# Moving two small side tasks of a fused attention and expert kernel on TensorE's slots, and two small VectorE operations in another form

## The reference, cut to what matters

```python
x = x + xattn(ctx, layernorm(x))   # q, k, v projections; 32 sub-heads of 8 dims; softmax over 128 keys
#   att = softmax(q k / sqrt(8)); att = att[:, :, 0] - lam * att[:, :, 1]; out = att @ v
x = x + moe(layernorm(x))
#   shared = silu(x @ ws_gate) * (x @ ws_up) @ ws_down
#   scores = sigmoid(x @ gate_w.T); top 2, weights normalised and times 2.5
#   routed = sum over the two chosen experts of weight * (silu(x @ w_gate) * (x @ w_up)) @ w_down
```

## Time and profile before

| | |
|---|---|
| median of 3 runs | 2349.24 us (2347.07 to 2359.59) |
| the profiled execution's own time | 2360.34 us |
| its span, first to last instruction | 2358.6 us |
| busy: TensorE, VectorE, ScalarE, GpSimd | 86%, 70%, 62%, 59% of the span |
| mean granted TensorE clock | 0.96 |

### The profile page before, as it was taken

One profiled execution on the slowest core, in us unless ns is written; L12 is line 12 of the kernel. 1 busy time (PEld: TensorE's weight loads), 2 busy tenths in 40 slices (PEclk: granted clock), 3 DMA queues, 4 the chain that ended last, 5 costly groups with the idle time before them and its releaser, 6 DMA issues.

```text
span 2358.6 us, 76415 instructions
## 1 busy us (share of the span) xinstructions
PE 2039.5 (86%) x20269; PEld 1421.1 (60%) x20270; DVE 1653.8 (70%) x4770; ACT 1464.0 (62%) x3558; POOL 1381.4 (59%) x2121
## 2 busy tenths in 40 slices
PE   4888888888888889888888888888883799989997
PEld 3555565555555556555555555555552677768886
DVE  3667777788878887888788887888763566644443
ACT  2666666767777777777677776767651344435553
POOL 4355666666666666666666666666643355545665
PEclk8799999999999999999999999999986899989999
DMA  4566556656566656656566565656534799867784
GB/s 136 168 205 195 164 161 166 169 161 173 164 174 170 170 169 170 175 163 171 165 177 167 165 171 166 175 165 172 154 89 152 250 290 293 284 215 237 233 244 144
DMA packets 583280, 432.50 MB, mean 183 GB/s; under 512 B 434070, under 2 KB 507930, under 8 KB 582688
## 3 DMA queue, kind: packets, MB, share of 16 engines
q1 hardware_dynamic: 547872, 342.28, 52.7%
q0 software_dynamic: 30720, 84.99, 9.9%
q10 hardware_dynamic: 4608, 4.26, 0.5%
HBM read 235.18 MB, written 200.47 MB: 185 GB/s over the span
## 4 chain that ended last, share of the span: by engine, by line
PE 52%; DVE 17%; issue 14%; SPq 5%; DMA 5%; ACT 4%; ACTq 1%; DVEq 1%; POOL 1%; POOLq 0%
PE mx_ps L715 9%; PE mx_ps L469 7%; PE ms_ps L551 6%; PE ms_ps L728 5%; DVE mx L917 4%; PE ms_ps L530 4%; PE o_ps L502 4%; PE st_ps L707 3%; DVE mxp L924 3%; DMA stacks<-mxT 2%; PE ms_ps L531 2%; ACT rowt L758 2%; PE ms_ps L532 2%; PE o_ps L513 2%; PE ms_ps L559 2%
## 5 line engine op out<-in xcount | busy, mean ns | idle before, releaser
L917 DVE TENSOR_REDUCE mx<-mx_ps 128x4 f32<-128x512 f32 x1024 | 701.6, 686 | 301.1 <-PE mx_ps L469 291.3
L776 ACT ACTIVATE prob<-st_ps 128x512 f32<-128x512 f32 x1024 | 609.1, 603 | 428.1 <-PE st_ps L462 426.2
L469 PE MATMUL mx_ps<-stacks 48*128 48x128 bf16 x4096 | 400.7, 222 | 34.1 <-DMA stacks<-mxT 24.6
L462 PE MATMUL st_ps<-stacks 50*128 50x128 bf16 x4096 | 397.4, 221 | 0.0
L469 PEld LDWEIGHTS mx_ps<-stacks 48*128 48x128 bf16 x4096 | 233.0, 96 | 196.1 <-issue 104.6
L502 PE MATMUL o_ps<-prob,v_sb 128*32 128x256 f32 x4096 | 330.8, 395 | 1.2 <-ACT oT L767 0.8
L715 PE MATMUL mx_ps<-w_gu_sb,prob 128*128 x1152 | 301.9, 385 | 0.0
L1122 DVE TENSOR_TENSOR prob<-prob,mx_ps 128x128 f32<-128x128 f32 x288 | 83.0, 288 | 221.3 <-ACT prob L859 219.7
L462 PEld LDWEIGHTS st_ps<-stacks 50*128 50x128 bf16 x4096 | 231.4, 95 | 2.2 <-issue 1.1
L1313 POOL DMA_INDIRECT rows_dram<-stacks x144 | 141.5, 983 | 154.2 <-DVE stacks L1116 142.8
L854 ACT ACTIVATE prob<-st_ps 128x256 f32<-128x256 f32 x288 | 110.4, 383 | 159.2 <-PE st_ps L707 152.9
(11 more groups left out here) (199 smaller groups left out, 4948.7 us busy)
## 6 DMA issues: line engine op xcount, KB each, us to landing
stacks<-stack_dram SPq DMA_DIRECT2D x512, 192.0 KB
stacks<-rows_dram SPq DMA_DIRECT2D x144, 260.0 KB
stack_dram<-kp SPq DMA_DIRECT2D x128, 256.0 KB, 3.0
stack_dram<-qp SPq DMA_DIRECT2D x64, 384.0 KB, 3.8
stacks<-rows_dram SPq DMA_DIRECT2D x144, 132.0 KB
stacks<-base_dram SPq DMA_DIRECT2D x144, 128.0 KB
x_in<-in_x SPq DMA_DIRECT2D x64, 256.0 KB
c_in<-in_ctxT SPq DMA_DIRECT2D x64, 256.0 KB, 2.7
```

Source lines behind the costliest of these rows:

```text
L462: return pe.matmul(st_ps[k % 2][:, i * P:(i + 1) * P], k_st[p][64 * h:64 * h + KROWS, u, j, :], q_st[p][64 * h:64 * h + KROWS, u, j, :], s ...
L469: return pe.matmul(mx_ps[k % 2][:, i * P:(i + 1) * P], q_st[p][64 * h:64 * h + ROWS, u, j, :], k_st[p][64 * h:64 * h + ROWS, u, j, :], sta ...
L776: nc.scalar.activation(prob[k % 4][:, :], st_ps[k % 2][:, :], ACT.Exp, scale=float(HALF) ** -0.5).then_inc(a_exp, 1)
L917: v.tensor_reduce(mx[:, u, c * CHUNK:(c + 1) * CHUNK], mx_ps[k % 2][:, :].rearrange("p (c n) -> p c n", c=CHUNK), AX.X, ALU.max).then_inc( ...
```

## The change

Rank sums go from bank TO in slot 9 to bank M0 in slot 11; for that the first half of the key projection goes from slot 11 to slot 13. The turn of the second maxima goes from slot 1 to the end of slot 2, that of the first maxima from slot 11 to slot 10, with ScalarE's copy of the second moved to k = 2 and the tanh of the shared expert from k = 6 to k = 5. VectorE does `places` at k = 12 and `positions` at k = 13 (before 10 and 11); the copy to bf16 becomes a maximum over an axis of length one, and the place of a row a sum of absolute values straight from `hotp`. On GpSimd the query's `split` comes before the first two scatters. SyncE's list is unchanged.

```diff
--- before.py
+++ after.py
@@ -563,9 +563,10 @@
             def clear(it, bank, n):
 
                 a, b, d, r = it.plus(3), it.plus(1), it.plus(-1), it.plus(-2)
-                users = {"M0": (((a_v, 1, b, 1),), ((a_e, 1, r, 1),), ((a_dn, 1, r, 1),), ((a_k, 2, a, 2),)),
+                users = {"M0": (((a_v, 1, b, 1),), ((a_e, 1, r, 1),), ((a_dn, 1, r, 1),), ((v_pf, 1, r, 1),),
+                                ((a_k, 2, a, 2),)),
                          "M1": (((v_x, 1, a, 1),), ((v_sh, 1, r, 1),), ((v_q, 1, a, 1),), ((a_h, 1, d, 1),)),
-                         "TO": (((a_mT, 2, it, 2),), ((v_cb, 4, d, 4),), ((v_cb, 4, it, 1),), ((v_pf, 1, r, 1),),
+                         "TO": (((a_mT, 2, it, 2),), ((v_cb, 4, d, 4),), ((v_cb, 4, it, 1),),
                                 ((a_mT, 2, b, 1),), ((v_cb, 4, it, 2),), ((v_cb, 4, it, 3),))}[bank]
                 for i, user in enumerate(users):
                     if it.k is None or i == (n - 1) % len(users):
@@ -579,15 +580,15 @@
                     clear(it, "M1", 0)
                     wait(pe, a_n1, 2, a, 2)
                     turn(xn, M1, p_xT)
-                if k == 1 and do_c:
-                    clear(it, "TO", 0)
-                    turn_max(it, 1)
                 if k in (1, 2) and do_b:
                     if k == 1:
                         clear(it, "M0", 0)
                     mm = value(b, k - 1)
                     if k == 2:
                         mm.then_inc(p_v, 1)
+                if k == 2 and do_c:
+                    clear(it, "TO", 0)
+                    turn_max(it, 1)
                 if k in (3, 5) and do_r:
                     if k == 3:
                         clear(it, "M1", 1)
@@ -603,7 +604,7 @@
                     turn_out(d, 3)
                 if k in TURN_AT and do_c:
                     h = TURN_AT.index(k)
-                    clear(it, "TO", (2, 5, 6)[h])
+                    clear(it, "TO", (2, 4, 5)[h])
                     turn_out(it, h)
                 if k in (8, 9) and do_r:
                     if k == 8:
@@ -620,20 +621,20 @@
                     mm = project(0, (x_hi, x_lo), M1, k - 9)
                     if k == 10:
                         mm.then_inc(p_q, 1)
-                if k == 9 and do_r:
+                if k == 10 and do_b:
                     clear(it, "TO", 3)
+                    turn_max(b, 0)
+                if k == 11 and do_r:
+                    clear(it, "M0", 3)
                     wait(pe, v_hot, 1, r, 1)
                     flat = hot[:, :, :, :].rearrange("p u k e -> p (u k e)")
-                    pe.matmul(TO[:, 0:2 * E2], upper[:, :], flat, start=True, stop=True)
-                    pe.matmul(TO[:, 2 * E2:4 * E2], onesb[:, :], flat, start=True, stop=True).then_inc(p_pf, 1)
-                if k == 11 and do_b:
-                    clear(it, "TO", 4)
-                    turn_max(b, 0)
-                if k in (11, 14) and do_a:
-                    if k == 11:
-                        clear(it, "M0", 3)
+                    pe.matmul(M0[:, 0:2 * E2], upper[:, :], flat, start=True, stop=True)
+                    pe.matmul(M0[:, 2 * E2:4 * E2], onesb[:, :], flat, start=True, stop=True).then_inc(p_pf, 1)
+                if k in (13, 14) and do_a:
+                    if k == 13:
+                        clear(it, "M0", 4)
                         wait(pe, g_cl, 1, a, 1)
-                    mm = project(1, (c_hi[a.par()], c_lo[a.par()]), M0, (k - 11) // 3)
+                    mm = project(1, (c_hi[a.par()], c_lo[a.par()]), M0, k - 13)
                     if k == 14:
                         mm.then_inc(p_k, 1)
                 if k == 13 and do_d:
@@ -799,7 +800,7 @@
                         nc.scalar.activation(kp[:, 1, :], k_rest[:, :], ACT.Copy).then_inc(a_kb, 1)
                     if k == 5 and do_c:
                         copy_out(it, 0)
-                    if k == 6 and do_r:
+                    if k == 5 and do_r:
                         wait(act, p_su, 1, r, 1)
                         wait(act, v_sg, 1, r)
                         nc.scalar.activation(sh_t[:, :], M1[:, 0:SW], ACT.Tanh, scale=0.5).then_inc(a_sh, 1)
@@ -921,7 +922,8 @@
 
                     wait(dve, v_red, NCH, s, k + 1)
                     wait(dve, p_mT, 2, s)
-                    v.tensor_copy(mxp[:, u, :, 0, :], mx[:, u, :].rearrange("p (h j) -> p h j", h=2)).then_inc(v_mxa, 1)
+                    v.tensor_reduce(mxp[:, u, :, 0, :], mx[:, u, :].rearrange("p (h j one) -> p h j one", h=2, one=1), AX.X,
+                                    ALU.max).then_inc(v_mxa, 1)
                     wait(dve, v_mxa, 1, s, 1)
                     v.tensor_tensor(mxp[:, u, :, 1, :], mx[:, u, :].rearrange("p (h j) -> p h j", h=2), mxp[:, u, :, 0, :],
                                     ALU.subtract).then_inc(v_mx, 1)
@@ -981,9 +983,9 @@
 
 
                 row = rowt[s.par()]
-                tot = TO[:, 2 * E2:4 * E2].rearrange("p (u e) -> p u e", u=2)
-                place = TO[:, 0:2 * E2]
-                both, safe, part = (TO[:, 4 * E2 + 2 * i:4 * E2 + 2 * i + 2] for i in range(3))
+                tot = M0[:, 2 * E2:4 * E2].rearrange("p (u e) -> p u e", u=2)
+                place = M0[:, 0:2 * E2]
+                both, safe, part = (M0[:, 4 * E2 + 2 * i:4 * E2 + 2 * i + 2] for i in range(3))
                 wait(dve, p_pf, 1, s, 1)
                 v.tensor_reduce(both, top[:, :, 0:TOPK], AX.X, ALU.add).then_inc(v_rt, 1)
                 v.tensor_tensor(base[:, 1, :], base[:, 0, :], tot[:, 0, :], ALU.add).then_inc(v_ps, 1)
@@ -1006,11 +1008,12 @@
             def positions(s):
                 row = rowt[s.par()]
                 wait(dve, v_ps, 3, s, 3)
-                v.tensor_reduce(row[:, :, C_POS:C_POS + TOPK], hotp[:, :, :, :], AX.X, ALU.add).then_inc(v_w, 1)
-                wait(dve, v_w, 1, s, 1)
+                v.tensor_reduce(row[:, :, C_POS:C_POS + TOPK], hotp[:, :, :, :], AX.X, ALU.add,
+                                apply_absolute_value=True).then_inc(v_w, 1)
                 wait_par(dve, d_scat, SCAT, s.plus(-2))
-                v.scalar_tensor_tensor(posi[s.par()][:, :], row[:, :, C_POS], -1.0, row[:, :, C_POS], ALU.mult,
-                                       ALU.max).then_inc(v_pos, 1)
+                with nc.allow_low_precision(reason="one place among zeros, a whole number below 2**24"):
+                    v.tensor_reduce(posi[s.par()][:, :], hotp[:, :, 0, :], AX.X, ALU.add,
+                                    apply_absolute_value=True).then_inc(v_pos, 1)
 
             def step(it):
                 a, b, d, xs, r = it.plus(3), it.plus(1), it.plus(-1), it.plus(4), it.plus(-2)
@@ -1038,12 +1041,12 @@
                     if k == 9 and do_d:
                         wait(dve, g_x2, 4, d, 4)
                         stats(d, x2[d.par()], bs2, mv2, v_b2, v_s2, a_n2)
-                    if k == 10 and do_r:
+                    if k == 12 and do_r:
                         places(r)
-                    if k == 11 and do_r:
-                        positions(r)
                     if k == 12 and do_a:
                         rest(a, M1, a_q, qp, q_rest, g_qs, v_q)
+                    if k == 13 and do_r:
+                        positions(r)
 
             steps(dve, step)
 
@@ -1285,15 +1288,16 @@
                     numbers(r)
                 if do_c:
                     residual(it, 0)
+                if do_a:
+                    split(a, q_rest, qp, a_qb, g_qs)
                 if do_r:
                     wait(gp, v_pos, 1, r, 1)
                     wait(gp, v_pf, 1, r, 1)
+                    wait(gp, v_w, 1, r, 1)
                     wait(gp, g_tok, 1, r, -1)
                     scatter(r, 0, 1)
                     wait(gp, g_base, 1, r, 1)
                     scatter(r, 0, 0)
-                if do_a:
-                    split(a, q_rest, qp, a_qb, g_qs)
                 if do_c:
                     residual(it, 1)
                 if do_r:
```

## The result

The changed kernel takes 2523.59 us (median of four, 2509.99 to 2534.66) against 2349.06 us before (four, 2347.07 to 2359.59): 1.073 times as long, 95% interval [1.067, 1.079]. That is 174.5 us more, where I had forecast 94 more, and 3.6 us above my range. Its profiled execution took 2525.35 us, with a span of 2523.6 and a mean granted clock of 0.90 (before 0.96).

A forecast was written before the change was run, and what follows sets the result against it. TensorE's and SyncE's chains were taken as tied; after the change SyncE's sets the period: 4.5 + 23.0 = 27.5 us, plus 0.8 for the clock, 28.3. That is 1.6 us more in 59 iterations: 2349 + 94 = 2443 us, range 2325 to 2520.

The forecast's parts named there:

- The two tied chains: TensorE's work and SyncE's in-order queue close the same loop at nearly equal length; the longer sets the period, 26.6 us.
- the costly one: Second maxima's turn moved to just before slot 3: everything in SyncE's list comes 1.1 us later.
- SyncE's chain at 23.0 us from copy to landing: From ScalarE's copy of the second maxima to the landing of slot 0's last DMA: 23.0 us.
- The copy at 4.5 us with the clock up: ScalarE's copy of the second maxima ends 4.5 us after slot 0 instead of 3.4.
- The clock: One large idle time ahead of slot 0 lowers TensorE's granted clock: 0.8 us per iteration, bounds 0 and 2.7.
- the sum 27.5 + 0.8: Forecast period: 4.5 us to the copy plus 23.0 of SyncE's chain, plus 0.8 for the clock, 28.3 us.
- TensorE alone at 24.3 us: TensorE's own period: 26.7 us less 3.0 of removed waits, plus 0.6 for new ones.
- VectorE's forms: Reduces at L924 and L1012 take about 0.2 us each, saving VectorE 1.1 and 0.8; nothing for the period.
- Rival 2: SyncE's chain has room, TensorE bounds: 2207 us in full, 2278 to 2331 partly; chance 0.19.
- rival 3: No change: SyncE's chain of 22.1 to 22.4 us, period 26.6 to 26.9; chance 0.11.
- rival 4: VectorE's reduce is held up as the cast was: VectorE alters by 1.1 us, the period not; no chance given.
- Rival 1: SyncE's chain bounds and the clock does not fall: 26.9 to 27.5 us per iteration, 2360 to 2396 us; chance 0.20.

The follow-up runs named there:

- e1: Changed kernel with the turn of the second maxima and ScalarE's copy back in slot 1 (k = 1): 2403.51 us, 0.976 of before.
- e2: Kernel before with only the turn of the second maxima moved to the end of slot 2, ScalarE's copy at k = 2: 2526.92 us, 1.026 of before.
- e4: Changed kernel with SyncE's list reordered, second maxima's DMAs between the query and key puts: 2319.94 us, 0.947 of before.
- e4b: Repeat of the changed kernel with SyncE's list reordered: 2301.40 us, 0.936 of before.
- f3: Changed kernel with SyncE's list reordered, beside the changed kernel on one long chip: 2323.27 us, 0.944 of before, 0.907 of the changed kernel.
- e7: Changed kernel with SyncE's list reordered and the turn of the second maxima back in slot 1: 2348.58 us, 0.952 of before.
- e6: Changed kernel with the cast to bf16 back in place of the reduce: 2560.71 us, 1.035 of before.
- f2: Changed kernel plus 44 unused matmuls ahead of slot 0 in each iteration: 2451.92 us, 0.997 of before, 0.957 of the changed kernel.
- f1: Changed kernel run again, unaltered, on a long chip: 2562.42 us, 1.042 of before.
- run 11: Not a label: the words say that the kernel before, unaltered, was profiled in an execution 11 us over its median, at 2360.3 us.
- e5: Kernel before with only the cast of the maxima to bf16 replaced by the reduce: 0.986 of before.

## Why the prediction was right or wrong

**The two tied chains: right.** Taking TensorE's waits away alone would have made the kernel faster; SyncE's chain set the period. e1 and e2 put the loss on the turn of the second maxima, the edit called the costly one, and e4, e4b and f3 show that it acts through SyncE's list: with the list changed, the changed kernel is faster than before, and e7 finds that the move by itself then gains 0.4 to 0.5 us a pass.

**SyncE's chain at 23.0 us from copy to landing: right to 0.4.** It measured 22.64 (22.42 before). It is the same in e1, e2, e6 and f2, 21.95 to 22.5, whatever the copy's time, as a chain of issues and landings should be. I had leaned towards the 23.8 of a pass whose last DMA took 6.58 us.

**The copy at 4.5 us with the clock up: right to 0.25.** 4.75 in the passes of f2 without half clock, and 4.50 in the best. Then 4.75 + 22.4 is 27.2; those passes of f2 take 27.48, and the chain without the clock had been put at 27.5.

**The clock: this is the step that failed.** The text took 0.8 us, "many iterations lose about 1.5, some nothing". The runs showed 1.7 to 1.9. None loses nothing: all 49 passes of f1 run at half clock for part of their first 7 us. The copy is 1.9 us later by it (6.67 against 4.75) and the period 1.7 to 1.9 (29.38 against 27.71 for all passes of f2 or 27.44 for those without a fall). In the sum 27.5 + 0.8, the first term came out at 27.4 (4.75 and 22.64) and the second at 1.7 to 2.1 (29.48 less 27.4 is 2.1). The bounds of 0 to 2.7 held it, but the value I took was near the low end, and the range ended at a loss of 2 us a pass. The period itself, 29.48, lies just inside that end (29.6, or 2520 us); the median went 3.6 us beyond it by what the runs scatter. Of the 174.5 us that came, the forecast had 94.

The forecast had said itself that TensorE would idle for 3 us, and the nearest row of the trace to that was the 2.37 us ahead of 180.41, after which slots 0 to 2 took 6.87 us instead of about 4.1, 2.7 us more. I weighed the row at 1.36 us against it, which was farther from 3 than 2.37 is. It was also no safe row: in the same trace the fall in the pass from 1303.65 starts at 1307.14, behind a wait of 1.28 us in slot 1, and four more of the six falls between 200 and 1650 us come behind waits of 1.0 to 1.3 us there. So "shorter idle times did less" held for one place and not for the other. Going by the nearest row, the sum would have been 27.5 + 2.7 = 30.2 us, 0.7 too much, where mine was 1.2 too little; no row that I read pointed to the value between them.

The Trainium skill (TensorE: Matmul & The Clock Gate, Part 1) has activity release the throttle; f2 agrees, where matmuls that compute nothing of use kept the clock up and won 4.3% of the changed kernel's time.

In time: 29.48 less 26.71 is 2.77 us, by 59 passes 163 us. The last slot 0 came 161.8 us later (1839.8 against 1678.0), and behind it 3.2 us were added (683.8 against 680.6): 165.0 us between the two spans. The kernel before had its profile in a run 11 us over its median, the changed one 2 us over, and that makes up the difference to the 174.5 of the medians.

**TensorE alone at 24.3 us: not reached by any run.** The nearest is f3 with 25.5, of which 1.8 us a pass are waits (83.2 us in the 47 passes of the stretch, 9.2 of them in two smaller rows that are not shown). The 0.6 us allowed for new waits would not have been enough there.

**VectorE's forms.** The place of a row takes 0.18 instead of 1.05: the number was right, but I had put the 1.05 down to the operation, and the trace of the kernel before shows a hold there too:

```profile
1005.82 1.29 POOL L1213 TENSOR_TENSOR rowt<-sh_o,x 128x512 f32<-128x512 f32 x1
1006.07 1.05 DVE L1012 SCALAR_TENSOR_TENSOR posi<-rowt 128x2 uint32<-128x2 f32 x1
```

Beside GpSimd's `shared_add` it ends at 1007.12, that one at 1007.11. In 62 of the 64 passes the two ends lie 14 to 22 ns apart; in the other two they don't overlap, and the operation takes 0.16 us. The reduce of the maxima takes 0.19. That the subtraction would inherit the hold, which the text named as a possibility and as what the Trainium skill's rule (SBUF — State Buffer, Who interferes with whom) gives, is what e5 shows where a split runs beside it: 0.98 instead of 0.38. In the changed kernel neither operation is held, and e6 (2560.71, against 2562.42 on another long chip) agrees with the sum, in which the exchange is worth nothing.

**Rivals.** Rival 2 (room in the chain) and rival 3 (no change) are out by the waits; rival 4 by the 186 ns. Rival 1, SyncE's chain and no fall of the clock (26.9 to 27.5 us), is what the 44 passes of f2 without half clock at their start show, at 27.48.

## What to carry to other kernels

A wait that is removed from an engine is worth having only if what it fed is not made later; before an operation is moved behind others, look for who stands in an in-order queue behind its result, here seven puts and six loads that did not need it. Then repair the queue first: with the list reordered, the same change runs at 0.94 to 0.95 of the kernel before on the long chips, the fastest version measured; its ratio on a quick chip was not taken, and an estimate from the periods (25.5 against 26.7 us, by 59 passes 71 us) makes the lead 3% there. And when several short waits of TensorE are about to become one long one, price the clock from the row whose idle time is nearest to the one expected, as a cost in every pass, and see whether the slowed stretch feeds the chain that sets the period. That row gave 0.7 us too much here; the average over milder ones gave 1.2 too little.

## What the runs showed that I had not expected

- **Chips differ, and not evenly.** The kernel before took 2355 us on one chip and 2457 to 2466 on three. The changed kernel took 2527 on the quick one and 2562 on a long one. The reordered list took 2301 to 2323 on the long chips, where before takes 135 to 165 us more. A ratio taken on one chip did not hold on another (1.072 and 1.042, intervals apart). In the first stage the granted clock was at half for 82 us against 17, and VectorE took up the second maxima 1.3 us later; which of the two led to the other, and what lies behind them, no run shows.
- **The clock turned into latency.** Half clock adds work time to TensorE, but the loss came as a longer way to the copy, ahead of 22.5 us that the clock doesn't touch. In the kernel before, on the long chip, where TensorE was busy or in short waits for the whole pass, a pass with a fall took 1.5 us more on average (26.99 to 28.51); here the loss was as large with TensorE idle for 3.4 us in the same pass.
- **Added work made the kernel faster.** 44 matmuls of 128 columns in each pass took 110 us off the changed kernel (2562.42 to 2451.92).
- **A hold moves on to the next operation.** With the cast gone, the subtraction took the wait (0.38 to 0.98 us); with GpSimd's split elsewhere, the same cast took 0.18 us. The 1.05 us of the place of a row were such a hold too, by another GpSimd operation.
